# Splitting the two triangular row passes of the first mixer between VectorE and GpSimd

## The chip, the cores and the metric

The kernel runs on one core of one Trainium2 chip. The metric is the device time of one execution in microseconds, the median of several executions. The engines named below are TensorE (PE), VectorE (DVE), ScalarE (ACT), GpSimd (POOL) and the DMA queue of SyncE (SP).

## The reference, cut to what matters

The model is two layers of a mixer and a mixture of experts on a 1024 x 256 activation. Only the first mixer matters here, a delta rule over 512 tokens, 2 batches and 16 heads of 16 channels:

```
q = _l2norm(q) * Dk ** (-0.5)
k = _l2norm(k)
def step(S, inp):
    qt, kt, vt, bt = inp
    u = vt - einsum('bhk,bhkv->bhv', kt, S)
    S = S + bt[:, :, None, None] * kt[..., :, None] * u[..., None, :]
    o = einsum('bhk,bhkv->bhv', qt, S)
_, o = jax.lax.scan(step, S0, (qT, kT, vT, bT))
```

The output is normalised per head, gated, multiplied with `Wo` and added to `x`. Then come the experts of layer 0, an attention with 16 heads of 128 channels, and the experts of layer 1.

## The kernel before

The delta rule is computed in chunks of CH = 16 tokens. Inside a chunk the recurrence is a triangular system. Its matrices are built from products of the chunk's keys and queries (`grams`, TensorE) and turned so that the 128 partitions hold batch, tile and head, and the free dimension holds 8 chunks and the 16 x 16 entries. `scale_a` (L2760, VectorE) writes the scaled key-key entries `aul` from PSUM; ScalarE writes the query-key entries `pul` and the diagonal of the second matrix (L2439, L2446).

Then VectorE solves row by row:

- T is `ful[0]`. For i = 0 to 14, a multiplication (L2780) writes the products of column i of `aul` with row i of T into `tmp[0]`, and a subtraction (L2794) takes them from rows i+1 to 15. Each works on (15-i) x 8 x (i+1) elements per partition, between 120 and 512.
- The second matrix is `ful[1]`. For z = 1 to 15, a multiplication (L2788) writes the products of column z of `pul` with row z of T into `tmp[1]`, and an addition (L2798) adds them to rows z to 15, on (16-z) x 8 x z elements. Step z needs T's row z, which is final after T's step z-1.

The loop over m in `dve` runs T's step m and the second matrix's step m-2 together, as four instructions. An operand of all of them and the result lie in SBUF (`arena`, and `w` for the `tmp` buffers); none touches PSUM. `s_el` counts them, with the targets in `el_t` and `el_z`. Among the first three steps stand four pairs of `scale_a` and two `rke` (L2720); these read a PSUM bank and one SBUF operand.

TensorE meanwhile works through a written order: `turn_ft(i)` (L2251) turns four rows of T (i even) or of the second matrix (i odd) to the front, between the sums (L2131) and four `gates` (L2241). ScalarE takes the turned rows out (`ft_out`, L2469). `turn_ft(7)` needs the last row of the second matrix. Behind it VectorE copies two rows (L2805), and then VectorE, ScalarE and GpSimd spread the matrices (`spread`, L2820, L2501, L2645), TensorE forms `units` (L2287), and a serial chain over NCH = 32 chunks of the state follows (L2314, L2330, L2868), with no slack between its engines.

GpSimd's queue in that stretch holds, in this order: the clearing of `ful` (L2600, L2602), the scaling of `wo0` (L2610), the clearing of 4096 elements at XO (L2612, `s_qz`, on which 16 DMAs of SP wait, L2098), `hdiag` and `seed`, the chain's first state, in 16 small copies (L2614 to L2620), `wz` (L2626), two clearings that wait for the last gate (L2630, L2631), and the spreads.

Of the kernel before, what the change touches and what calls it, by code (L numbers as in the profile page):

```python
# [7 lines left out]
P = 128  # L8
# [3 lines left out]
KD = DIM // P  # L12
# [4 lines left out]
H0, D0, CONV = 16, 16, 4  # L17
CH = 16
# [34 lines left out]
ALU = mybir.AluOpType  # L53
# [1838 lines left out]
def make_attn0(nc, io, sem, sb, arena, bank, rest, g):  # L1892
# [14 lines left out]
    def at(off, n):  # L1907
        assert off + n <= ARENA
        return arena[:, off:off + n]
# [6 lines left out]
    XO = 10240 + 2 * XYW  # L1916
# [68 lines left out]
    s_el = sem("a0_el")  # L1985
    s_qz = sem("a0_qz")
# [90 lines left out]
    el_t, el_z, el_n = {}, {}, 0  # L2077
    for m in range(CH + 2):
        el_n += (m < CH - 1) + (1 <= m - 2)
        if m < CH - 1:  # L2080
            el_n += 1
            el_t[m] = el_n
        if 1 <= m - 2:
            el_n += 1
            el_z[m - 2] = el_n

    class Attn0:
# [12 lines left out]
        def pe(self, pe):  # L2100
# [144 lines left out]
            def turn_ft(i):  # L2245
                y, r0 = i % 2, i // 2 * 4
                pe.wait_ge(s_el, el_z[r0 + 3] if y else el_t[r0 + 2])
# [327 lines left out]
        def pool(self, pool):  # L2575
# [32 lines left out]
            pool.wait_ge(s_const.sem, n_const)  # L2608
            for k in range(KD):
                nc.gpsimd.tensor_scalar(wo0[:, k, :], wo0[:, k, :], norm_w[:, 0:1], 1.0, ALU.mult, ALU.mult).then_inc(s_one, 1)  # L2610
            pool.wait_ge(s_ut, 8)
            pool.memset(at(XO, 4096), 0.0).then_inc(s_qz, 1)  # L2612
# [75 lines left out]
        def dve(self, dve):  # L2688
# [78 lines left out]
            for m in range(CH + 2):  # L2767
                i, z = m, m - 2
                if m < 4:
                    scale_a(2 * m)  # L2770
                    scale_a(2 * m + 1)
                    if m in (1, 2):
                        rke(m + 1)
                    dve.wait_ge(s_ua, 2 * m + 2)
                if i < CH - 1:
                    n, w = CH - 1 - i, i + 1
                    tt = tmp[0][:, 0:n * 8 * w].rearrange("p (r c j) -> p r c j", r=n, c=8)
                    if m:
                        dve.wait_ge(s_el, el_t[m - 1])
                    nc.vector.tensor_tensor(tt, aul[:, i, :, i + 1:CH].rearrange("p c r -> p r c").unsqueeze(3).to_broadcast([P, n, 8, w]),  # L2780
                                            ful[0][:, i, :, 0:w].unsqueeze(1).to_broadcast([P, n, 8, w]),
                                            ALU.mult).then_inc(s_el, 1)
                if z >= 1:
                    nz = CH - z
                    tz = tmp[1][:, 0:nz * 8 * z].rearrange("p (r c j) -> p r c j", r=nz, c=8)
                    dve.wait_ge(s_el, el_z[z - 1] if z > 1 else el_t[z - 1])
                    dve.wait_ge(s_uz, 3 * (z // 4) + 3)
                    nc.vector.tensor_tensor(tz, pul[:, z, :, z:CH].rearrange("p c r -> p r c").unsqueeze(3).to_broadcast([P, nz, 8, z]),  # L2788
                                            ful[0][:, z, :, 0:z].unsqueeze(1).to_broadcast([P, nz, 8, z]),
                                            ALU.mult).then_inc(s_el, 1)  # L2790
                if i < CH - 1:
# [199 lines left out]
```

## Time and profile before

| what | us |
|---|---|
| median of 3 runs | 836.53 (835.92 to 839.29) |
| the profiled execution, its time | 836.49 |
| its span, first to last instruction | 834.7 |
| VectorE busy in the span | 482.1 |
| GpSimd busy in the span | 218.4 |
| mean granted TensorE clock | 0.991 |

All rows come from one profiled execution. A timeline row gives start, duration, engine, line of the kernel, operation, result and operands, their shapes and the count of merged instructions, and in brackets the idle time of the engine ahead of it with what ended it. A row of a windows view gives the stretch, its length, the busy time with the count in brackets, the granted TensorE clock as a share of 2.4 GHz, and DMA.

### The profile page before, as it was taken

How to read it: one execution, taken by the hardware profiler on the slowest of the kernel's cores; microseconds unless marked ns; L12 is line 12 of the kernel's file. 1: busy time of each engine (PE TensorE's matmuls, PEld its weight loads, DVE VectorE, ACT ScalarE, POOL GpSimd, SP SyncE). 2: the span in 40 equal slices, each digit the busy share in tenths (PEclk: the TensorE clock that was granted, in tenths of full speed). 3: DMA queues.
4: the chain of work that ended last, by engine and by line, in shares of the span. 5: the costliest groups of instructions: out<-in, count | busy, mean ns of one | idle time of the engine just before them, and what ended most of it. 6: DMA issues, size and time to landing. Idle time of an engine off the chain costs nothing.

```text
span 834.7 us, 14393 instructions
## 1 busy us (share of the span) xinstructions
PE 787.2 (94%) x4825; PEld 545.6 (65%) x4825; DVE 482.1 (58%) x1167; ACT 360.4 (43%) x755; POOL 218.4 (26%) x318
## 2 busy tenths in 40 slices
PE   5988799879989998899999999999999999999998
PEld 3576566665657776577777777777764545455557
DVE  5999866766622225865564575967645463324443
ACT  3988777646213324343323343232347666211111
POOL 3644654111610015111211211217712333200000
PEclk9998999999999999999999999999999999999999
DMA  4001790083343312034443232223333433284431
GB/s 145 2 1 29 220 309 1 3 209 101 102 139 103 106 60 82 13 103 135 122 131 93 69 102 69 61 54 99 119 71 114 141 96 110 88 278 126 127 126 50
DMA packets 95807, 85.72 MB, mean 103 GB/s; under 512 B 34792, under 2 KB 84456, under 8 KB 95736
## 3 DMA queue, kind: packets, MB, share of 16 engines
q1 hardware_dynamic: 88200, 70.05, 28.9%
q0 software_dynamic: 4224, 11.74, 4.0%
q10 hardware_dynamic: 3312, 3.02, 1.1%
q8 instruction: 41, 0.67, 0.3%
q14 instruction: 30, 0.25, 0.1%
HBM read 57.02 MB, written 26.71 MB: 100 GB/s over the span
## 4 chain that ended last, share of the span: by engine, by line
PE 79%; DVE 10%; ACT 6%; issue 3%; DMA 1%; SPq 1%; POOL 0%; ACTq 0%; DVEq 0%; POOLq 0%
PE bank L1502 9%; PE bank L1461 8%; PE bank L1320 7%; PE bank L1359 7%; PE bank L1345 6%; PE bank L1281 6%; PE bank L1297 6%; PE bank L744 4%; PE bank L770 3%; PE bank L967 3%; PE bank L2330 3%; PE bank L989 2%; ACT arena L2387 2%; PE bank L2287 2%; PE bank L2314 2%
## 5 line engine op out<-in xcount | busy, mean ns | idle before, releaser
L1619 ACT ACTIVATE arena<-bank 128x512 f32<-128x512 f32 (+1 forms) x96 | 46.8, 525 | 142.7 <-PE bank L1461 142.7
L1243 POOL TENSOR_TENSOR arena<-arena,causal_t 128x256 f32<-128x256 f32 x64 | 45.3, 729 | 208.5 <-ACT arena L1624 207.5
L1502 PEld LDWEIGHTS bank<-arena 128*128 128x128 f32 x640 | 76.2, 191 | 3.9 <-POOL arena L1243 2.3
L1502 PE MATMUL bank<-arena 128*128 128x129 f32 x640 | 77.0, 275 | 1.5 <-POOL arena L1243 1.5
L1461 PE MATMUL bank<-arena 128*128 128x512 f32 (+3 forms) x256 | 74.5, 434 | 1.4 <-DVE arena L1697 1.4
L1554 ACT ACTIVATE arena<-bank 128x512 f32<-128x512 f32 (+1 forms) x39 | 20.2, 520 | 120.7 <-PE bank L1281 111.9
L1320 PE MATMUL bank<-arena 128*128 128x256 f32 (+1 forms) x272 | 66.2, 382 | 3.5 <-DVE arena L1677 3.4
L1281 PE MATMUL bank<-xnT,arena 128*128 128x512 f32 (+1 forms) x168 | 65.9, 514 | 0.0
L1320 PEld LDWEIGHTS bank<-arena 128*128 128x128 f32 (+1 forms) x272 | 50.9, 190 | 21.8 <-issue 10.8
L1359 PEld LDWEIGHTS bank<-arena 128*128 128x128 f32 x256 | 48.3, 190 | 21.6 <-issue 13.6
L1359 PE MATMUL bank<-arena 128*128 128x256 f32 x256 | 60.8, 380 | 1.4 <-issue 0.9
L1345 PE MATMUL bank<-arena 128*128 128x512 f32 x128 | 60.5, 595 | 1.2 <-DVE arena L1695 0.8
L1297 PE MATMUL bank<-xnT,arena 128*128 128x512 f32 (+1 forms) x156 | 61.5, 516 | 0.0
L1461 PEld LDWEIGHTS bank<-arena 128*128 128x128 f32 x256 | 41.3, 191 | 27.0 <-issue 18.5
L1679 DVE TENSOR_TENSOR arena<-arena,bank 128x512 f32<-128x512 f32 (+1 forms) x25 | 15.6, 623 | 68.0 <-PE bank L1297 68.0
L851 POOL DMA_INDIRECT ret<-arena,ridx x32 | 30.7, 960 | 77.0 <-ACT arena L818 60.3
L1693 DVE TENSOR_TENSOR arena<-bank,arena 64x512 f32<-64x512 f32 x36 | 25.0, 693 | 36.7 <-PE bank L1345 26.2
L1297 PEld LDWEIGHTS bank<-xnT,arena 128*128 128x128 f32 x156 | 29.6, 190 | 25.3 <-issue 23.8
L744 PE MATMUL bank<-arena 128*64 (+1 forms) x256 | 44.9, 472 | 0.0
L1704 DVE COPY arena<-bank 128x256 f32<-128x256 f32 x64 | 24.1, 418 | 34.5 <-PE bank L1369 30.8
L2330 PE MATMUL bank<-w,arena 128*128 128x128 f32 x248 | 35.5, 286 | 7.2 <-DVE w L2863 3.3
L1281 PEld LDWEIGHTS bank<-xnT,arena 128*128 128x128 f32 x168 | 31.2, 190 | 16.5 <-issue 14.0
(297 smaller groups left out, 1489.6 us busy)
## 6 DMA issues: line engine op xcount, KB each, us to landing
arena<-in_w_gu SPq DMA_DIRECT2D x44, 256.0 KB, 3.3
rows_in<-place SPq DMA_DIRECT2D x5, 1664.0 KB, 14.6
arena<-in_w_dn SPq DMA_DIRECT2D x34, 128.0 KB, 3.5
rows<-arena SPq DMA_DIRECT2D x8, 544.0 KB, 4.4
arena<-in_w_dn SPq DMA_DIRECT2D x24, 176.0 KB
arena<-in_wq SPq DMA_DIRECT2D x32, 128.0 KB
arena<-in_wo SPq DMA_DIRECT2D x32, 128.0 KB
arena<-rows SPq DMA_DIRECT2D x32, 128.0 KB, 2.0
```

What stands on the lines that cost most here:

```text
L744: mm = nc.tensor.matmul(p_gu[J % 2][u * HR:(u + 1) * HR, 0:2 * FE].rearrange("p (y n) -> p y n", y=2), pxT[:, J % 2, k, u * HR:(u + 1) * H ...
L851: nc.gpsimd.indirect_dma_start(ret[h], bass.IndirectOffsetOnAxis(ap=ridx[:, h, j:j + 1], axis=0), py[J % NY], None).then_inc(s_ret, 16)
L1243: nc.gpsimd.tensor_tensor(blocks, blocks, causal_t[:].unsqueeze(1).to_broadcast([P, 2, P]), ALU.mult).then_inc(s_p, 1)
L1281: mm = nc.tensor.matmul(ring(M)[0][:, 0:n], (w_gu, w_gu1)[s][:, slot_of(M), k * P:(k + 1) * P], xnT[:, k, cols], start=(k == 0), stop=(k = ...
L1297: mm = nc.tensor.matmul(ring(M)[1][:, 0:n], (w_gu, w_gu1)[s][:, slot_of(M), (KD + k) * P:(KD + k + 1) * P], xnT[:, k, cols], start=(k == 0 ...
L1320: mm = nc.tensor.matmul(Y[s][half][l // 2][:, (l % 2) * DIM:(l % 2 + 1) * DIM], (hh, hh1)[s][rows, M % 3, j * P:(j + 1) * P], (w_dn, w_dn1 ...
L1345: mm = nc.tensor.matmul(b_q[:], wq[:, n % 2, k, :], xnT2[:, k, b * SEQ:(b + 1) * SEQ], start=(k == 0), stop=(k == KD - 1))
L1359: mm = nc.tensor.matmul(b_y[t // 2][:, (t % 2) * DIM:(t % 2 + 1) * DIM], oT[:, t * P:(t + 1) * P], wo[:, n % 2, :], start=first and t % 2 ...
L1461: mm = nc.tensor.matmul(b_s[sbank][:, o:o + w], kT[:, grp, kt * P:(kt + 1) * P], qr[:, kt * P:SEQ], start=True, stop=True, skip_group_chec ...
L1502: mm = nc.tensor.matmul(b_o[pair][:, t * (DH + 1):(t + 1) * (DH + 1)], pr[:, o:o + P], v[:, grp, kt, :], start=(kt == 0), stop=(kt == qb))
L1619: nc.scalar.activation(th[:, sbank * 512:sbank * 512 + w], b_s[sbank][:, 0:w], ACT.Tanh, scale=SCALE / SOFTCAP).then_inc(s_th, 1)
L2330: mm = nc.tensor.matmul(sacc[h][:, j * P:(j + 1) * P], kq[:, u, hq * P:(hq + 1) * P], ub[s][:, hq, :], start=False, stop=True, skip_group_ ...
```

## The change

VectorE runs all 15 steps of T first and then steps z = 8 to 15 of the second matrix. GpSimd runs steps z = 1 to 7, each as soon as T's row z is final, counted by the new semaphore `s_ez`. TensorE's `turn_ft(1)` and `turn_ft(3)` wait on `s_ez`. On GpSimd's queue, `hdiag` and `seed` move ahead of these steps and `seed` is made by 4 copies of 32 x 64 elements; the clearing at XO and the scaling of `wo0` move behind them.

```diff
-    el_t, el_z, el_n = {}, {}, 0
+    ZP = 7
+    el_t = {m: 2 * (m + 1) for m in range(CH - 1)}
+    el_z = {z: 2 * (CH - 1) + 2 * (z - ZP) for z in range(ZP + 1, CH)}
+    el_n = el_z[CH - 1]
...
             def turn_ft(i):
                 y, r0 = i % 2, i // 2 * 4
-                pe.wait_ge(s_el, el_z[r0 + 3] if y else el_t[r0 + 2])
+                if y and r0 + 3 <= ZP:
+                    pe.wait_ge(s_ez, 2 * (r0 + 3))
+                else:
+                    pe.wait_ge(s_el, el_z[r0 + 3] if y else el_t[r0 + 2])
...
-            pool.wait_ge(s_const.sem, n_const)
-            for k in range(KD):
-                nc.gpsimd.tensor_scalar(wo0[:, k, :], wo0[:, k, :], norm_w[:, 0:1], 1.0, ALU.mult, ALU.mult).then_inc(s_one, 1)
-            pool.wait_ge(s_ut, 8)
-            pool.memset(at(XO, 4096), 0.0).then_inc(s_qz, 1)
+            pool.wait_ge(s_pp, 12)
...
-                for x in range(4):
-                    ins = nc.gpsimd.tensor_copy(seed[rows, x * 64 + h * D0:x * 64 + (h + 1) * D0],
-                                                ident[rows, 32 * h + D0:32 * h + 32])
+                ins = nc.gpsimd.tensor_copy(seed[rows].rearrange("p (x h d) -> p x h d", x=4, d=D0)[:, :, h, :],
+                                            ident[rows, 32 * h + D0:32 * h + 32].unsqueeze(1).to_broadcast([32, 4, D0]))
             ins.then_inc(s_seed, 1)
+            pool.wait_ge(s_seed, 1)
+            for z in range(1, ZP + 1):
+                nz = CH - z
+                tz = tmp[1][:, 0:nz * 8 * z].rearrange("p (r c j) -> p r c j", r=nz, c=8)
+                pool.wait_ge(s_el, el_t[z - 1])
+                pool.wait_ge(s_uz, 3 * (z // 4) + 3)
+                if z > 1:
+                    pool.wait_ge(s_ez, 2 * (z - 1))
+                nc.gpsimd.tensor_tensor(tz, pul[:, z, :, z:CH].rearrange("p c r -> p r c").unsqueeze(3).to_broadcast([P, nz, 8, z]),
+                                        ful[0][:, z, :, 0:z].unsqueeze(1).to_broadcast([P, nz, 8, z]),
+                                        ALU.mult).then_inc(s_ez, 1)
+                pool.wait_ge(s_ez, 2 * z - 1)
+                dst = ful[1][:, z:CH, :, 0:z]
+                nc.gpsimd.tensor_tensor(dst, dst, tz, ALU.add).then_inc(s_ez, 1)
+            pool.wait_ge(s_ut, 8)
+            pool.memset(at(XO, 4096), 0.0).then_inc(s_qz, 1)
+            pool.wait_ge(s_const.sem, n_const)
+            for k in range(KD):
+                nc.gpsimd.tensor_scalar(wo0[:, k, :], wo0[:, k, :], norm_w[:, 0:1], 1.0, ALU.mult, ALU.mult).then_inc(s_one, 1)
```

In `dve` the loop over m becomes a loop over i with T's two instructions, then a wait for `s_ez` at 14 and for `s_uz` at 12, and a loop over z from 8 with the second matrix's two.

VectorE, where T's step 8 stood beside the second matrix's step 6, before: `arena` operands are `aul`, `pul` and `ful`, `w` is `tmp`.

```order
L2780 TENSOR_TENSOR w<-arena 128x504 [waits a0_el]
L2788 TENSOR_TENSOR w<-arena 128x480 [waits a0_uz,a0_el]
L2794 TENSOR_TENSOR arena<-arena,w 128x56x9 [waits a0_el]
L2798 TENSOR_TENSOR arena<-arena,w 128x80x6 [waits a0_el]
L2780 TENSOR_TENSOR w<-arena 128x480 [waits a0_el]
```

The same place after, and the turn from T's last step to the second matrix's step 8:

```order
L2791 TENSOR_TENSOR w<-arena 128x504 [waits a0_el]
L2796 TENSOR_TENSOR arena<-arena,w 128x56x9 [waits a0_el]
L2791 TENSOR_TENSOR w<-arena 128x480 [waits a0_el]
...
L2796 TENSOR_TENSOR arena<-arena,w 128x8x15 [waits a0_el]
L2803 TENSOR_TENSOR w<-arena 128x512 [waits a0_el,a0_uz,a0_ez]
L2808 TENSOR_TENSOR arena<-arena,w 128x64x8 [waits a0_el]
```

The pairs of two passes became one pass behind the other, and each instruction now waits for the one ahead of it. 14 instructions left VectorE.

GpSimd, from the scaling of `wo0` to the clearing of `ub`, before:

```order
L2610 TENSOR_SCALAR wo<-wo,norm_w 128x256 [waits s_const]
L2610 TENSOR_SCALAR wo<-wo,norm_w 128x256
L2612 MEMSET arena 128x4096 [waits a0_ut]
L2613 MEMSET hdiag 128x64
...
L2620 COPY w<-ident 32x16 x4
L2626 TENSOR_TENSOR wz<-kn,beta 128x128 [waits a0_srk,a0_rk,a0_seed]
L2630 MEMSET w 128x1024 [waits a0_g,a0_b,a0_srk]
```

After, from the last copy of `seed` on:

```order
L2614 COPY w<-ident 32x4x16
L2625 TENSOR_TENSOR w<-arena 128x120 [waits a0_uz,a0_el,a0_seed]
L2630 TENSOR_TENSOR arena<-arena,w 128x120 [waits a0_ez]
...
L2625 TENSOR_TENSOR w<-arena 128x504 [waits a0_ez,a0_uz,a0_el]
L2630 TENSOR_TENSOR arena<-arena,w 128x72x7 [waits a0_ez]
L2632 MEMSET arena 128x4096 [waits a0_ut]
L2635 TENSOR_SCALAR wo<-wo,norm_w 128x256 [waits s_const]
L2635 TENSOR_SCALAR wo<-wo,norm_w 128x256
L2639 TENSOR_TENSOR wz<-kn,beta 128x128 [waits a0_srk,a0_rk,a0_seed]
L2643 MEMSET w 128x1024 [waits a0_g,a0_b,a0_srk]
```

Fourteen two-operand instructions now stand ahead of the clearing at XO, and the scaling of `wo0` stands behind both.

## Rows read from the trace of the kernel before

**Rows 1.** The page: the chain that ended last, shares of the span by engine.
```profile
PE 79%; DVE 10%; ACT 6%; issue 3%; DMA 1%; SPq 1%; POOL 0%; ACTq 0%; DVEq 0%; POOLq 0%
```

**Rows 2.** The chain that ended last: start, us, what; from the solve's end to the units.
```profile
90.08 0.67 PE bank L2251 x4
...
90.77 0.60 DVE arena L2805
...
91.92 1.34 DVE arena L2820 x3
...
93.58 1.07 PE bank L2287 x16
...
97.98 1.11 PE bank L2287 x16
```

**Rows 3.** Windows view of VectorE: L2780, L2794, then the last eight of L2788.
```profile
62.20:90.10 27.90, 7.05 (x12) 0.88 0.24 39
...
62.20:90.10 27.90, 6.91 (x12) 0.88 0.24 39
...
77.45:90.10 12.65, 4.33 (x8) 0.80 0.52 84
```

**Rows 4.** Timeline of VectorE in the solve.
```profile
62.23 0.56 DVE L2780 TENSOR_TENSOR w<-arena 128x384 f32<-128x384 f32 x1
...
65.65 0.65 DVE L2780 TENSOR_TENSOR w<-arena 128x480 f32<-128x480 f32 x1
...
74.78 0.92 DVE L2780 TENSOR_TENSOR w<-arena 128x480 f32<-128x480 f32 x1
...
87.53 0.48 DVE L2788 TENSOR_TENSOR w<-arena 128x312 f32<-128x312 f32 x1
88.05 0.48 DVE L2798 TENSOR_TENSOR arena<-arena,w 128x312 f32<-128x312 f32 x1
```

**Rows 5.** Timeline of GpSimd beside the solve.
```profile
52.91 0.93 POOL L2610 TENSOR_SCALAR wo<-wo,norm_w 128x256 f32<-128x256 f32 x2
59.73 3.52 POOL L2612 MEMSET arena<- 128x4096 f32 x1 [5.89 <-PE bank L2196]
...
69.09 2.14 POOL L2620 COPY w<-ident 32x16 f32<-32x16 f32 x4
74.57 0.61 POOL L2626 TENSOR_TENSOR wz<-kn,beta 128x128 f32<-128x128 f32 x1 [3.35 <-ACT kn L2459]
```

**Rows 6.** Timeline near 197 us, VectorE first, then GpSimd.
```profile
196.99 0.89 DVE L575 TENSOR_TENSOR arena<-arena 128x32 f32<-128x32 f32 x1
197.92 0.43 DVE L582 TENSOR_TENSOR arena<-arena 128x256 f32<-128x256 f32 x1
198.38 1.38 DVE L585 TENSOR_TENSOR arena<-arena 128x256 f32<-128x256 f32 x1
...
196.78 1.06 POOL L2661 TENSOR_TENSOR arena<-arena 128x512 f32<-128x512 f32 x1 [2.28 <-DVE arena L2901]
197.91 1.56 POOL L2665 TENSOR_TENSOR arena<-arena,xn 128x512 f32<-128x512 f32 x1
```

**Rows 7.** Timelines of TensorE, ScalarE and SP's queue at the solve's end.
```profile
88.82 1.04 PE L2251 MATMUL bank<-ident,arena 128*128 128x128 f32 x8
...
89.52 2.37 ACT L2469 COPY arena<-bank 128x512 f32<-128x512 f32 x3
...
76.72 10.70 SPq L2098 DMA_DIRECT2D arena<-arena  x16
```

**Rows 8.** Windows view: PE, PEld, DVE, ACT, POOL busy, PEclk, DMA share, GB/s.
```profile
48.00:52.00 4.00, 2.11 (x56) 1.75 (x59) 3.86 (x8) 3.98 (x9) 1.97 (x2) 0.97 0.02 4
52.00:56.00 4.00, 4.00 (x38) 3.62 (x31) 3.76 (x8) 2.52 (x4) 1.79 (x19) 0.60 0.01 2
...
76.00:80.00 4.00, 4.00 (x19) 3.95 (x20) 3.93 (x8) 2.69 (x5) 0.00 (x0) 0.50 0.37 56
...
96.00:100.00 4.00, 2.14 (x32) 1.00 (x32) 3.74 (x14) 2.59 (x9) 4.00 (x8) 1.00 1.05 354
```

More of the change, by code:

```diff
@@ L1985, in make_attn0 @@
     s_el = sem("a0_el")
+    s_ez = sem("a0_ez")
     s_qz = sem("a0_qz")
@@ L2073, in xy_from @@
         return xy_bank(i)[:].rearrange("p (q y v c i) -> p q y v c i", q=2, y=2, v=2, c=4)[:, :, y, :, :, :]
-    el_t, el_z, el_n = {}, {}, 0
[L2078 to L2085, printed above, removed]
+    ZP = 7
+    el_t = {m: 2 * (m + 1) for m in range(CH - 1)}
+    el_z = {z: 2 * (CH - 1) + 2 * (z - ZP) for z in range(ZP + 1, CH)}
+    el_n = el_z[CH - 1]
     class Attn0:
@@ L2766, in dve @@
             dve.wait_ge(s_pz, 4)
[L2767 to L2791, printed above, removed]
-                    dve.wait_ge(s_el, el_t[m] - (1 if z >= 1 else 0) - 0 - (0 if z >= 1 else 1))
-                    dst = ful[0][:, i + 1:CH, :, 0:w]
-                    nc.vector.tensor_tensor(dst, dst, tt, ALU.subtract).then_inc(s_el, 1)
-                if z >= 1:
-                    dve.wait_ge(s_el, el_z[z] - 1 - (1 if i < CH - 1 else 0))
-                    dst = ful[1][:, z:CH, :, 0:z]
-                    nc.vector.tensor_tensor(dst, dst, tz, ALU.add).then_inc(s_el, 1)
@@ new lines, in dve @@
+            for i in range(CH - 1):
+                if i < 4:
+                    scale_a(2 * i)
+                    scale_a(2 * i + 1)
+                    if i in (1, 2):
+                        rke(i + 1)
+                    dve.wait_ge(s_ua, 2 * i + 2)
+                n, w = CH - 1 - i, i + 1
+                tt = tmp[0][:, 0:n * 8 * w].rearrange("p (r c j) -> p r c j", r=n, c=8)
+                if i:
+                    dve.wait_ge(s_el, el_t[i - 1])
+                nc.vector.tensor_tensor(tt, aul[:, i, :, i + 1:CH].rearrange("p c r -> p r c").unsqueeze(3).to_broadcast([P, n, 8, w]),
+                                        ful[0][:, i, :, 0:w].unsqueeze(1).to_broadcast([P, n, 8, w]),
+                                        ALU.mult).then_inc(s_el, 1)
+                dve.wait_ge(s_el, el_t[i] - 1)
+                dst = ful[0][:, i + 1:CH, :, 0:w]
+                nc.vector.tensor_tensor(dst, dst, tt, ALU.subtract).then_inc(s_el, 1)
@@ new lines, in dve @@
+            dve.wait_ge(s_ez, 2 * ZP)
+            dve.wait_ge(s_uz, 12)
+            for z in range(ZP + 1, CH):
+                nz = CH - z
+                tz = tmp[1][:, 0:nz * 8 * z].rearrange("p (r c j) -> p r c j", r=nz, c=8)
+                dve.wait_ge(s_el, el_z[z] - 2)
+                nc.vector.tensor_tensor(tz, pul[:, z, :, z:CH].rearrange("p c r -> p r c").unsqueeze(3).to_broadcast([P, nz, 8, z]),
+                                        ful[0][:, z, :, 0:z].unsqueeze(1).to_broadcast([P, nz, 8, z]),
+                                        ALU.mult).then_inc(s_el, 1)
+                dve.wait_ge(s_el, el_z[z] - 1)
+                dst = ful[1][:, z:CH, :, 0:z]
+                nc.vector.tensor_tensor(dst, dst, tz, ALU.add).then_inc(s_el, 1)
```

## The prediction, written before the change was timed

> **What bounds the kernel now.** I read the shares of the chain of waits first, then the chain between 86 and 101 us, and then the timelines of the engines there. TensorE holds 79% of the chain [rows 1], but not in this stretch: between 62 and 90 us VectorE steps through the solve almost without a pause. Of 27.9 us from the first four-instruction step at 62.23 on, all but a few tenths are its instructions [rows 3, 4]. The reader should see in the chain how the solve ends: TensorE's last turn starts at 90.08, right behind the last addition; VectorE's copy of two rows follows, and the spreads start at 91.92 [rows 2]. From there the units and the serial chain of the state follow, so what these spreads gain or lose the kernel gains or loses in full.
>
> Just under that chain lies a second one. TensorE's turns 5 and 6 run at 88.82, behind the last gate, and ScalarE's last three copies run from 89.52 to 91.89 without a pause [rows 7]. The spreads wait for the third. So if VectorE ended its solve several us sooner, these two engines would still hold the spreads at about 91.9. This caps any gain at about nothing.
>
> **VectorE's own work after the change.** From 62.23 on, twelve steps of T are left. Their multiplications took 7.05 us, of which one was lengthened from 0.65 to 0.92 (below), so 6.78; the subtractions took 6.91 [rows 3, 4]. Two instructions that depend on each other start 0.04 us after the other's end (87.53 and 0.48, then 88.05) [rows 4], and now all do: 24 x 0.04 = 0.96. T would end at 62.23 + 6.78 + 6.91 + 0.96 = 76.9. Steps 8 to 15 of the second matrix: 4.33 us for the multiplications, as much for the additions, 16 x 0.04 of gaps, 9.3 together [rows 3]. That gives 86.2 with nothing in the way, against 90.0 before: 3.8 us less. The 14 instructions that left held more than that, but the interleaved order let independent ones overlap, and this is lost.
>
> **What stands in the way: GpSimd's reads.** Twice the trace shows VectorE reading two SBUF operands while GpSimd does so too. At 74.57 GpSimd multiplied 128 elements for `wz`, and the multiplication of 480 elements beside it took 0.92 instead of 0.65 us [rows 4, 5]: 0.27 us, or 2.1 ns per element of GpSimd's. At 197.91 GpSimd ran 512 elements, and VectorE's 256 elements took 1.38 us [rows 6], where the 256 just ahead of them took 0.43: 0.95 us, or 1.9 ns per element. At 196.99 VectorE's 32 elements took 0.89 and ended with GpSimd's 512 [rows 6]. From 0.43 for 256 and 0.65 for 480 I estimate 0.2 for 32 elements alone, so it stood for 0.7 us, 1.4 ns per element, a lower bound since GpSimd had started before. So VectorE stands for nearly the time in which GpSimd works, rather than sharing. The copies of 32 x 16 elements did it no visible harm though they took longer themselves (0.53 us each in the last four) [rows 5]; they are too small to serve as a price.
>
> The moved steps have 120 + 224 + 312 + 384 + 440 + 480 + 504 = 2464 elements, twice: 4928. At 1.9 ns that is 9.4 us. I take 1.9 and not 2.1 because the 512-element row is the nearer one in size. The first three of the fourteen (464 elements, 0.9 us) can run beside `scale_a` and `rke`, which read PSUM and one SBUF operand; I take 1.1 off with a part of the fourth. The rest meets T: from z = 4 on, each GpSimd instruction finds a VectorE one beside it, and both take turns. This leaves **8.3 us**. Bounds: 1.4 ns gives 6.7 - 0.7 = 6.0; 3.0 ns, the whole of the 1.56 us for 512 elements [rows 6], gives 15.0 - 1.4 = 13.6.
>
> The Trainium skill ("SBUF — State Buffer", section "Who interferes with whom") says that a VectorE instruction with two SBUF inputs contends with a GpSimd instruction that reads SBUF, and that the second to start fully blocks until the first is done. The rows above agree with the blocking, but charge somewhat less than the whole GpSimd instruction; by the letter of the page the sum would move toward the 13.6.
>
> **The rest of GpSimd's queue.** `hdiag` and `seed` run before the solve needs GpSimd: the scaling of `wo0` that stood there took 0.93 us [rows 5] and the moved items are writes and four small copies, some 2 to 2.5 us from 52.9, done by about 55.5, while `scale_a` and T's first step lie between there and 62.23. They cost nothing, and win nothing, since the chain uses `seed` first behind the spreads. The scaling of `wo0` now meets VectorE: two instructions of 256 elements with one operand, 0.93 together. I charge 0.6 (0 to 0.93). `wz` is charged its 0.27 as before. The clearing at XO (3.52 us, writes only) [rows 5] ended at 63.2 and will end at about 81: T's step 7 ends at 69 undisturbed and at about 77 with the charge, GpSimd's z = 7 with it. SP's 16 DMAs wait for it, 10.70 us from 76.72 on [rows 7], so they now run from 81 to 92 and have landed by 95; the first reader (L2832) stands behind the first units, which started at 93.58 and will start past 98. That is hidden, with some 4 us to spare. The waits on `s_ez` in turns 1 and 3 are met on time: turn 3 stands two gates of TensorE ahead of the turns at 88.82, and step 7 is done at about 77.
>
> **Sum.** 86.2 + 8.3 + 0.6 + 0.3 = 95.4 for the end of the solve. Turns 5 and 6 and their copies are then long done or nearly, so the tail is shorter: TensorE's last turn 0.05 + 0.67, VectorE's copy of two rows 0.60 [rows 2], spreads at 96.75. Before it was 91.92. **Later by 4.8 us.**
>
> **TensorE's clock.** Between 48 and 52 us TensorE was busy 2.11 of 4 us, and then the granted clock fell to half, 1.2 GHz (0.60 over the next stretch); between 76 and 80 it stood at 0.50 again. Between 96 and 100, with 2.14 of 4 busy, it did not fall [rows 8]. After the change TensorE has nothing from 89 to about 91.6 (turn 5 waits for z = 11), two turns, nothing to 95.4, one turn and the seed's products, and then the units: some 3 us of work in 9. That is less than ahead of the fall at 52, so I expect a fall at about 93 and the first units at half clock. The four groups of units start at 93.58 to 97.98 and take 1.07 each [rows 2]; at half clock they take 2.14, against a distance of about 1.5. Two slow groups cost 0.9 us, three 2.0; TensorE was slow for some 4 us after the fall at 52. **I take 1.5** (0 to 3).
>
> **Total**: 836.49 for the profiled execution + 4.8 + 1.5 = 842.8. The profiled execution lies 0.04 below the median of 836.53, so the sum stands for both. The forecast is 842.8 us, 0.75% slower.
>
> **Rivals.**
> - Reads collide, the clock holds. Same sum without the last term: 841.3. For it speaks the stretch at 96 to 100 us. At the low price of 1.4 ns it would be 839.0.
> - GpSimd's instructions block as a whole, or VectorE always goes first and GpSimd ends behind T. The first is 13.6 in place of 8.3: 846.6 with the clock still up, 848.1 with it down. The second: T ends at 76.9, GpSimd still has some 10 us of its 12 to do, and steps 8 to 15 add 9.3 after 87 to 88: the spreads start at about 98, or 843 to 844. The `wz` row speaks against it, since GpSimd got in there.
> - No collision worth the name. Then VectorE is done at 86.5, and the spreads wait for TensorE's turn 7, which comes right behind turns 5 and 6 at 89.86, and for ScalarE's last copy at 91.9. The time is 836.5. This is the case on the other side: the mechanism is that the shared work is hidden and TensorE and ScalarE become the bound. It decides if GpSimd's instructions hold VectorE for less than 91.2 - 86.5 = 4.7 us in all, about 1 ns per element. Against it stand three rows at 1.4 to 2.1 ns.
> - Faster by over 0.5% would need 4.2 us from somewhere in or behind the spreads. Nothing in the rows offers that.
>
> **How the numbers follow.** Forecast (collision, clock down) 0.46; clock holds 0.25; the larger price or GpSimd behind T 0.12; no collision 0.14; anything else, a gain among it, 0.03. About 0.5%, 4.2 us, is what a measurement of this kernel can tell from no change. The forecast's case lies above 840.7 nearly whole, the second for about two thirds, the third whole: slower 0.74. The no-collision case and the low end of the second give same 0.23, and faster has 0.03. The range of 838.0 to 848.0 leaves out the no-collision case, the remainder, and the top of the third, some 0.2 together; its low end takes in most of the lower price, its high end the whole-instruction price with the clock down.
>
> **What the changed profile would show.** Right: VectorE's T instructions between 62 and 77 us take 1.2 to 1.6 us each instead of 0.55 to 0.69, with GpSimd's fourteen of 0.4 to 1.6 us between them; T's last eight steps and steps 8 to 15 have the old durations; the spreads start near 96.8; SP's sixteen DMAs start near 81; the granted clock is at 0.5 somewhere between 92 and 102. Wrong: T's instructions keep their 0.55 to 0.69 (no collision), a wait of VectorE for GpSimd ahead of step 8 (GpSimd behind T), the first reader at XO waiting for a DMA, or a clock of 1.00 throughout. The forecast fails most easily in the price per element, since 0.5 ns in it are 2.5 us.

## The result: 0.45% slower

The changed kernel takes 840.11 us (median of 18 runs), the kernel before 835.39 us (18 runs). The ratio is 1.0045, 95% interval 1.0034 to 1.0055, or 3.8 us (2.8 to 4.6); the two medians by themselves lie 4.7 us apart, and I go by the ratio. One execution of the changed kernel took 1614.58 us, for a reason that the record does not show, and is left out of the ratio. The span of the profiled execution is 838.2 us, TensorE's mean granted clock 0.988. I had forecast 842.8 in a range of 838.0 to 848.0: the sign and the range held, and the sum was 2.5 us too high (6.3 us of loss instead of 3.8).

VectorE beside GpSimd, the timeline after, where steps 7 to 9 of T meet GpSimd's z = 6 and 7; then the end of the solve, the copy of two rows and the spreads. Columns as in [rows 4].

```profile
73.95 1.51 DVE L2791 TENSOR_TENSOR w<-arena 128x512 f32<-128x512 f32 x1
75.50 1.54 DVE L2796 TENSOR_TENSOR arena<-arena,w 128x512 f32<-128x512 f32 x1
77.07 1.54 DVE L2791 TENSOR_TENSOR w<-arena 128x504 f32<-128x504 f32 x1
78.65 0.68 DVE L2796 TENSOR_TENSOR arena<-arena,w 128x504 f32<-128x504 f32 x1
...
82.06 0.71 DVE L2791 TENSOR_TENSOR w<-arena 128x384 f32<-128x384 f32 x1
...
95.30 0.28 DVE L2808 TENSOR_TENSOR arena<-arena,w 128x120 f32<-128x120 f32 x1
...
96.79 0.65 DVE L2815 COPY arena<-bank 128x256 f32<-128x256 f32 x1 [0.54 <-PE bank L2250]
97.53 3.78 DVE L2830 TENSOR_SCALAR arena<-arena,headmask 128x256 f32<-128x256 f32 x9
101.51 1.33 DVE L2830 TENSOR_SCALAR arena<-arena,headmask 128x256 f32<-128x256 f32 x3 [0.20 <-PE bank L2286]
```

The same timeline for GpSimd; these rows answer to [rows 5].

```profile
56.48 0.24 POOL L2614 COPY w<-ident 32x64 f32<-32x64 f32 x1
...
75.08 1.41 POOL L2625 TENSOR_TENSOR w<-arena 128x504 f32<-128x504 f32 x1 [0.17 <-POOL arena L2630]
76.56 1.51 POOL L2630 TENSOR_TENSOR arena<-arena,w 128x504 f32<-128x504 f32 x1
78.01 3.52 POOL L2632 MEMSET arena<- 128x4096 f32 x1
81.50 1.62 POOL L2635 TENSOR_SCALAR wo<-wo,norm_w 128x256 f32<-128x256 f32 x2
```

The collision is plain. While GpSimd's multiplication and addition of 504 elements run, each of VectorE's instructions takes 1.51 to 1.54 us, as forecast (1.2 to 1.6). As soon as GpSimd goes over to a clearing, which reads nothing, the same 504 elements take 0.68. Beside the scaling of `wo0`, 384 elements take 0.71 instead of 0.56 [rows 4].

TensorE at the end of the solve, and SP's sixteen transfers; these answer to [rows 2, 7].

```profile
91.92 1.09 PE L2250 MATMUL bank<-ident,arena 128*128 128x128 f32 x8 [0.96 <-DVE arena L2808]
95.63 1.12 PE L2250 MATMUL bank<-ident,arena 128*128 128x128 f32 x4 [2.62 <-DVE arena L2808]
97.50 2.08 PE L2296 MATMUL bank<-w,ident 128*128 128x256 f32 x4 [0.75 <-ACT arena L2468]
99.50 4.53 PE L2286 MATMUL bank<-arena 128*32 128x256 f32 x64
105.54 0.69 PE L2313 MATMUL bank<-sh,arena 128*64 128x64 f32 x16 [1.50 <-DVE sh L2855]
```

```profile
81.56 10.69 SPq L2094 DMA_DIRECT2D arena<-arena  x16
```

The windows of that stretch after, which answer to [rows 8]:

```profile
92.00:96.00 4.00, 1.38 (x10) 1.14 (x11) 3.76 (x10) 1.93 (x2) 0.31 (x2) 0.81 0.22 37
96.00:100.00 4.00, 3.25 (x16) 1.79 (x18) 3.37 (x8) 3.14 (x8) 2.40 (x5) 0.50 0.51 137
100.00:104.00 4.00, 4.00 (x64) 1.89 (x56) 3.73 (x13) 3.34 (x10) 3.08 (x7) 0.83 0.97 314
```

TensorE's clock falls to half behind turn 6 and comes back inside the units: turn 7 takes 1.12 us instead of 0.67 [rows 2], the seed's products 2.08. That too was forecast. But from the first spread to the chain's first product at 105.54 it takes 8.01 us; before, it was 8.43 (100.35, the start of L2314 there, less 91.92 [rows 2]). The fall cost nothing there.

**Where the 3.8 us are.** The solve starts at a different moment in each profiled execution: the first pair of `scale_a` at 55.75 before, at 57.20 after. TensorE's clock falls near 50 us in both, but not at the same point of its work, and nothing that the change touches stands ahead of it. So I count from that pair. The pair before, then after:

```profile
55.75 0.81 DVE L2760 TENSOR_TENSOR arena<-bank,wul 128x256 f32<-128x256 f32 x2
...
57.20 0.74 DVE L2773 TENSOR_TENSOR arena<-bank,wul 128x256 f32<-128x256 f32 x2
```

| from the first `scale_a` pair to | before | after | difference | forecast |
|---|---|---|---|---|
| end of the solve | 34.27 | 38.38 | +4.1 | +5.4 |
| first spread | 36.17 | 40.33 | +4.2 | +4.8 |
| first product of the chain | 44.60 | 48.34 | +3.7 | +6.3 |
| first projection behind the layer (L1281) | 136.63 | 140.36 | +3.7 | +6.3 |

The difference is complete when the chain begins and stays to the layer's end; it is the 3.8 us of the ratio, within 0.1. The spans differ by 3.5 although the pair comes 1.45 us later after the change: what lies behind the layer took 642.3 us before and 640.6 after. That part varies by itself: it is 641.0 us in the repetition of the changed kernel (e9 below) and 642.5 in e1.

### The profile page after: what moved, and what is told of

The parts are those of the page before. It is cut to its first block, busy times and chain, and to the rows that moved or that the text cites. A ratio compares the mean times of both kernels' runs of the same rounds, so it can differ in the third digit from the quotient of the medians.

```text
span 838.2 us, 14374 instructions
## 1 busy us (share of the span) xinstructions
PE 789.9 (94%) x4825; PEld 547.4 (65%) x4825; DVE 485.3 (58%) x1153; ACT 360.8 (43%) x755; POOL 228.7 (27%) x320
## 4 chain that ended last, share of the span: by engine, by line
PE 78%; DVE 11%; ACT 5%; issue 3%; DMA 1%; SPq 0%; POOL 0%; ACTq 0%; DVEq 0%; POOLq 0%
PE bank L1502 9%; PE bank L1461 8%; PE bank L1320 7%; PE bank L1359 6%; PE bank L1345 6%; PE bank L1281 6%; PE bank L1297 6%; PE bank L744 4%; PE bank L770 3%; PE bank L967 3%; PE bank L2329 3%; PE bank L989 2%; PE bank L2286 2%; PE bank L2313 2%; PE bank L1369 2%
## 5 line engine op out<-in xcount | busy, mean ns | idle before, releaser
L1281 PE MATMUL bank<-xnT,arena 128*128 128x512 f32 (+1 forms) x168 | 65.9, 515 | 0.0
L1281 PEld LDWEIGHTS bank<-xnT,arena 128*128 128x128 f32 x168 | 31.3, 190 | 16.4 <-issue 13.9
```

The lines of the kernel that those rows point to most:

```text
L1281: mm = nc.tensor.matmul(ring(M)[0][:, 0:n], (w_gu, w_gu1)[s][:, slot_of(M), k * P:(k + 1) * P], xnT[:, k, cols], start=(k == 0), stop=(k = ...
```

## The experiments

Eleven kernels beside the changed one. "From pair to layer" is the last row of the table above, taken from each one's profiled execution.

| kernel | median us (runs) | kernel before, timed beside it | ratio, 95% interval | from pair to layer |
|---|---|---|---|---|
| changed | 840.11 (18) | 835.39 | 1.0045 (1.0034 to 1.0055) | 140.4 |
| e1_all_on_dve | 840.30 (10) | 835.62 | 1.0050 (1.0033 to 1.0067) | 140.1 |
| e2_write_only | 834.68 (10) | 835.62 | 0.9982 (0.9959 to 1.0005) | 136.5 |
| e3_pool_behind_T | 846.19 (2) | 835.62 | 1.0119 (1.0062 to 1.0176) | 147.4 |
| e4_products_in_psum | 836.90 (10) | 835.62 | 1.0010 (0.9991 to 1.0028) | 137.2 |
| e5_filled_clock | 847.27 (6) | 838.57 | 1.0091 (1.0063 to 1.0120) | 146.3 |
| e6_first_state_early | 837.76 (10) | 838.57 | 0.9982 (0.9953 to 1.0010) | 136.5 |
| e8_psum_interleaved | 837.05 (10) | 838.57 | 0.9981 (0.9957 to 1.0006) | 137.2 |
| e12_psum_interleaved_sums_early | 838.79 (10) | 838.57 | 1.0007 (0.9985 to 1.0029) | 137.1 |
| e9_changed_again | 838.51 (9) | 836.15 | 1.0031 (1.0013 to 1.0049) | 140.4 |
| e10_half_filler | 839.82 (4) | 836.15 | 1.0050 (1.0031 to 1.0069) | 140.5 |
| e11_interleaved | 838.79 (8) | 836.15 | 1.0031 (1.0015 to 1.0047) | 139.6 |

### Is it the collision, and how large is it?

**e1_all_on_dve**: the changed kernel without GpSimd's share.

```diff
-    ZP = 7
+    ZP = 0
-            dve.wait_ge(s_ez, 2 * ZP)
```

> VectorE runs T first and then all fifteen steps of the second matrix; GpSimd has none. Collision theory: nobody stands in the way, so T's steps from the fourth on take 14.7 us and the fifteen steps some 17.2 us (the 9.3 of steps 8 to 15, and 7.9 for steps 1 to 7); the solve ends some 4 us later than before and the spreads start 3.5 to 4 us later: the time is 3 to 4 us above before, the same as the changed kernel within 0.7 us, since what GpSimd took over came back as waiting. Rival (GpSimd's share is worth something and the loss of the changed kernel comes from the order or the clock): this kernel is 3 us or more slower than the changed one.

It costs what the changed kernel costs: 1.0050 against 1.0045. VectorE ends the solve at 95.28, 38.85 us after its pair, 0.5 later than in the changed kernel, though it has fourteen instructions more and no collision. So giving seven steps away bought 0.5 us at the solve's end, and nothing where the chain begins (48.10 us behind the pair in e1, 48.34 after the change).

e1 shows one thing more. VectorE runs the same sixty instructions of the solve as in the kernel before, only T first and the second matrix behind it, and ends 4.6 us later (38.85 against 34.27), since each instruction now waits for the one ahead of it. Some 0.3 us of this come from the scaling of `wo0`, which now stands beside the solve; the order itself costs some 4.3. So the 4.1 us by which the changed kernel ends its solve later are a sum: the new order costs 4.3, the small instructions of GpSimd 0.2, the fourteen instructions that left give back 8.0 (their time and gaps in e1, 78.05 to 86.03 us), and the collision, weighed below at 7.6, takes nearly all of that again. The collision is why the move did not pay; the loss against the kernel before is about as large as the price of the order.

**e2_write_only**: GpSimd's fourteen instructions become clearings of the same elements, so steps 1 to 7 of the second matrix are left out.

```diff
-                nc.gpsimd.tensor_tensor(tz, pul[:, z, :, z:CH].rearrange("p c r -> p r c").unsqueeze(3).to_broadcast([P, nz, 8, z]),
-                                        ful[0][:, z, :, 0:z].unsqueeze(1).to_broadcast([P, nz, 8, z]),
-                                        ALU.mult).then_inc(s_ez, 1)
+                nc.gpsimd.memset(tmp[1][:, 0:nz * 8 * z], 0.0).then_inc(s_ez, 1)
-                nc.gpsimd.tensor_tensor(dst, dst, tz, ALU.add).then_inc(s_ez, 1)
+                nc.gpsimd.memset(dst, 0.0).then_inc(s_ez, 1)
```

> The changed kernel with GpSimd's fourteen two-operand instructions replaced by clearings of the same shapes, which write and read nothing (the second matrix is left wrong by it). Collision by reads: T's instructions keep 0.28 to 0.69 us, the solve ends at about 87 us of the trace, TensorE's and ScalarE's chain of gates holds the spreads at about 92 plus whatever the start of the trace is late, and the time is that of before within 1 us. Rival (GpSimd's presence, its writes or its semaphores cost): T's instructions stay lengthened to over 1 us and the time stays 3 us or more above before.

Its timeline at the solve's end: VectorE, and ScalarE's last copies.

```profile
86.14 0.28 DVE L2806 TENSOR_TENSOR arena<-arena,w 128x120 f32<-128x120 f32 x1
...
89.98 0.58 DVE L2813 COPY arena<-bank 128x256 f32<-128x256 f32 x1 [2.89 <-PE bank L2250]
91.53 2.78 DVE L2828 TENSOR_SCALAR arena<-arena,headmask 128x256 f32<-128x256 f32 x6 [0.96 <-ACT arena L2468]
```

```profile
89.17 2.33 ACT L2468 COPY arena<-bank 128x512 f32<-128x512 f32 x3
```

Without GpSimd's reads VectorE is done 31 us after the pair (86.42 less 55.43), 7.4 us sooner than in the changed kernel, and then waits 2.89 us for TensorE and 0.96 us for ScalarE. The spreads start 36.1 us behind the pair, as in the kernel before (36.2). This is the rival "no collision" made real, and it gives the time that it gave: no change. So even a helper that did not hold VectorE up would have won nothing here, because TensorE's turns and ScalarE's copies end right behind.

**e3_pool_behind_T**: GpSimd waits until T is done.

```diff
-                pool.wait_ge(s_el, el_t[z - 1])
+                pool.wait_ge(s_el, el_t[CH - 2])
```

> GpSimd's steps wait until T is done, so neither engine reads SBUF beside the other. Collision theory: T's steps keep their old durations (14.7 us from the fourth on), and the fourteen GpSimd instructions show what they need alone: 0.2 us and 1.7 to 2.1 ns per element, some 12 to 13 us in all; VectorE waits for them, and the time is 7 to 9 us above before. If the lengthening in the changed kernel were slow GpSimd code and not waiting, the fourteen would take as long here as there (some 15.7 us).

GpSimd's last pair with nothing beside it, and VectorE's first instruction behind it:

```profile
90.44 1.16 POOL L2625 TENSOR_TENSOR w<-arena 128x504 f32<-128x504 f32 x1 [0.17 <-POOL arena L2630]
91.69 1.16 POOL L2630 TENSOR_TENSOR arena<-arena,w 128x504 f32<-128x504 f32 x1
```

```profile
92.88 0.69 DVE L2803 TENSOR_TENSOR w<-arena 128x512 f32<-128x512 f32 x1 [14.72 <-POOL arena L2630]
```

This weighs the collision. T's twelve steps from i = 3 take 14.55 us here (63.61 to 78.16), within 0.1 of the forecast's 14.65; in the changed kernel 21.92 (64.26 to 86.18). Of the 7.37 us between them, 0.31 belong to `wo0` and 0.14 to `wz`; some 0.64 more lie in steps 1 and 2, ahead of i = 3. So GpSimd's fourteen cost VectorE 7.6 us, or **1.5 ns per element of GpSimd's** (7.6 / 4928). GpSimd's own fourteen last 12.97 us alone and 15.67 in the changed kernel. VectorE therefore stood for somewhat over half of GpSimd's time: for 504 elements 0.85 us (1.54 less 0.69) of 1.16. GpSimd's 504 elements take 0.54 and 0.67 us more in e3 than its 120 (1.16 against 0.62 and 0.49). By my estimate its time so grows by 1.4 to 1.7 ns per element on top of a fixed 0.3 to 0.45 us, and the 1.5 ns that VectorE stood are about the growing part alone. The solve ends 7.0 us later than in the changed kernel, and the layer 7.0; I had expected 7 to 9 us over the kernel before and found 10: VectorE waits 14.72 us, not 12.97, since some 0.1 us pass between each two of GpSimd's dependent instructions, 1.75 us in all.

**e4_products_in_psum**: the work stays where the change put it, but T's products from i = 5 on lie in a free PSUM bank.

```diff
-                tt = tmp[0][:, 0:n * 8 * w].rearrange("p (r c j) -> p r c j", r=n, c=8)
+                tt = (bank[3] if i >= 5 else tmp[0])[:, 0:n * 8 * w].rearrange("p (r c j) -> p r c j", r=n, c=8)
+                if i == 5:
+                    dve.wait_ge(s_siv, KD + 4)
```

> The changed kernel, but T's products of steps 5 to 14 go to a PSUM bank. The subtractions then read one SBUF operand and one PSUM operand. Collision by two SBUF reads: the subtractions keep 0.6 to 0.7 us beside GpSimd, only the multiplications wait, and the delay from step 5 on falls from some 7 to 2 or 3 us: the time is 3 to 4 us under the changed kernel. Rival (any overlap of the two engines in SBUF costs, by writes or bandwidth): the subtractions stay at 1.3 to 1.5 us, and the time is the changed kernel's within 0.7 us.

VectorE in e4, and GpSimd beside it:

```profile
69.97 0.80 DVE L2793 TENSOR_TENSOR bank<-arena 128x504 f32<-128x504 f32 x1
70.81 0.68 DVE L2798 TENSOR_TENSOR arena<-arena,bank 128x504 f32<-128x504 f32 x1
71.52 0.76 DVE L2793 TENSOR_TENSOR bank<-arena 128x512 f32<-128x512 f32 x1
72.31 0.69 DVE L2798 TENSOR_TENSOR arena<-arena,bank 128x512 f32<-128x512 f32 x1
```

```profile
71.89 1.40 POOL L2625 TENSOR_TENSOR w<-arena 128x480 f32<-128x480 f32 x1 [0.17 <-POOL arena L2630]
73.37 1.47 POOL L2630 TENSOR_TENSOR arena<-arena,w 128x480 f32<-128x480 f32 x1
```

The subtraction of 512 elements takes 0.69 beside GpSimd, where it took 1.54, since one of its operands is in PSUM now. The multiplication still reads two operands in SBUF. The first one behind the change of place took 1.28 us (480 elements at 67.97), the later ones only 0.76 to 0.81. There VectorE's multiplication starts ahead of GpSimd's (71.52 against 71.89), so the two seem to have fallen into step. That this order is the reason is argued, not shown: GpSimd's 480 elements take 1.40 us here, but 1.38 in the changed kernel too, against 1.13 alone in e3. With the place of the products alone changed (the multiplication writes them, the subtraction reads them), 3.2 of the 3.7 us come back at the layer's end. At the solve's end it is somewhat over half of the collision: 34.16 us behind the pair, against 38.38 in the changed kernel and 30.99 in e2; the rest is hidden under ScalarE's copies (the last three run from 91.38 to 93.73, the first spread starts at 93.76). Together with e2, where GpSimd writes as much and VectorE is not held, this settles the cause: the reads collide, not the writes, the work or the waits. The Trainium skill ("SBUF — State Buffer", section "Who interferes with whom") says the same: an instruction of VectorE with at most one SBUF input, outside its two-port modes, does not contend with GpSimd (0.69 us here), and GpSimd only writing does not contend with two inputs either (e2). The page also calls the shared ports an exclusive lock; its sentence that the other engine is blocked for the whole instruction stands in that section for the two-port modes, and in the page's section "Terms" for the shared ports in general. For these instructions that is too strong in size: 0.85 of 1.16 us above, and in the changed kernel one instruction of VectorE's and one of GpSimd's pass every 1.5 to 1.6 us, less than the 0.69 and 1.16 that they take alone, 1.85 together.

### Does the fall of TensorE's clock cost anything?

**e5_filled_clock**: twenty products of the identity with itself between turns 6 and 7.

```diff
             for i in range(5, 8):
                 turn_ft(i)
+                if i == 6:
+                    for _ in range(20):
+                        nc.tensor.matmul(bank[3][:, 0:P], ident[:], ident[:], start=True, stop=True, skip_group_check=True)
```

> The changed kernel with 20 more TensorE matmuls of 128 columns into a bank nobody reads, between turns 6 and 7, so that TensorE isn't idle there. As the prediction had it (the clock's fall costs 1.5 us): the granted clock stays at 1.00 to the units, and the time is 1 to 2 us under the changed kernel. Rival, from comparing the traces of before and after (the units wait for the spreads, and spreads that start later collide less with GpSimd): the clock stays up, and the stretch from the spreads' start to the chain's first matmul is 8.4 us as before instead of 8.0, so the time is that of the changed kernel or up to 0.5 us above it.

TensorE in e5, then its windows in the chain:

```profile
91.54 4.63 PE L2268 MATMUL bank<-ident 128*128 128x128 f32 x40
96.01 0.60 PE L2250 MATMUL bank<-ident,arena 128*128 128x128 f32 x4
```

```profile
106.00:108.00 2.00, 2.00 (x32) 1.12 (x29) 0.88 (x3) 0.68 (x3) 2.00 (x5) 0.54 1.09 388
...
114.00:116.00 2.00, 2.00 (x12) 1.78 (x8) 0.42 (x1) 0.00 (x0) 0.00 (x0) 0.50 1.07 376
```

The filler was too long (4.63 us) and delayed turn 7 by itself. The clock then held through turn 7 and the units, and fell twice inside the chain instead, where every product is waited for: the chain took 96.3 us instead of 92. So this run says little of the fall ahead of the units and much of falls behind them: the two together cost some 4 us there. This is one execution, the slowest of the six (850.44 us). The filler was too large for the question; e10 below has half of it, with the changed kernel timed beside it.

**e9_changed_again**: the changed kernel once more.

> The changed kernel once more, beside the two kernels of this call and on their chip. Every theory expects what was measured: 3 to 4.5 us above the kernel before, the solve ending 5 to 6 us later after scale_a's start than before, turn 7 at half clock (1.1 us), and some 8 us from the first spread to the first product of the chain.

**e10_half_filler**: as e5 with `range(10)`.

> The changed kernel with 10 matmuls of 128 columns of the identity into a bank that is free, between turns 6 and 7 on TensorE. They take 2.3 us by the 4.63 us of twenty, and TensorE's pause there was 2.62 us, so turn 7 is not delayed as it was with twenty. Theory A, the fall of TensorE's clock ahead of the units costs 1.5 us of the time, as predicted: with the clock kept up this kernel is 1 to 1.5 us faster than the changed kernel of this call. Theory B, the units wait for the spreads and the fall costs at most turn 7's own 0.4 to 0.5 us: the time is that of the changed kernel within 0.5 us, and the stretch from the first spread to the chain's first product is as long as before (8.4 us) although the units run at full clock.

TensorE in e10 (each product is listed as two matmuls), from the filler to the chain's first product:

```profile
91.60 2.40 PE L2268 MATMUL bank<-ident 128*128 128x128 f32 x20
94.38 0.66 PE L2250 MATMUL bank<-ident,arena 128*128 128x128 f32 x4 [0.39 <-DVE arena L2811]
95.80 1.13 PE L2299 MATMUL bank<-w,ident 128*128 128x256 f32 x4 [0.76 <-ACT arena L2471]
97.50 2.29 PE L2289 MATMUL bank<-arena 128*32 128x256 f32 x32 [0.57 <-DVE arena L2833]
100.16 1.07 PE L2289 MATMUL bank<-arena 128*32 128x256 f32 x16 [0.38 <-issue]
101.90 1.07 PE L2289 MATMUL bank<-arena 128*32 128x256 f32 x16 [0.67 <-issue]
104.27 0.69 PE L2316 MATMUL bank<-sh,arena 128*64 128x64 f32 x16 [1.30 <-DVE sh L2858]
```

The changed kernel reproduced: 140.4 us from pair to layer, turn 7 in 1.11 us, 8.00 us from first spread to chain. In e10 the clock is 1.00 in every window from 90 to 116 us. Turn 7 is back at 0.66, and the stretch is back at 8.43: 0.45 won, 0.43 lost, and 140.5 us from pair to layer. Its ratio is no better than that of e9 (1.0050 against 1.0031, the intervals overlap), and its median of four runs is 1.3 us above e9's, more than the 0.5 us that theory B allowed; the traces do not show that difference, and theory A, which asked for 1 to 1.5 us less, is excluded. At full clock TensorE pauses 0.38 and 0.67 us between the groups of units. The profile names no releaser for these pauses, but VectorE's twelfth spread ends at 101.80 and the last group starts at 101.90, so it waits for the spreads. In the changed kernel these pauses are gone and the groups end no later for the chain. Why the stretch is even 0.4 us shorter then, I can only argue: VectorE's twelve spreads take 3.78 + 1.33 us in the changed kernel and 5.96 in e10, so they may collide less when the last three are held back, as they are there until the first group of units is done (`s_xy`).

### Parts of the change, and the order

**e6_first_state_early**: the kernel before with only GpSimd's queue in the new order: `hdiag` and `seed` (in four copies) ahead, the clearing at XO and the scaling of `wo0` behind.

```diff
+            pool.wait_ge(s_pp, 12)
+            nc.gpsimd.memset(hdiag[:], 0.0).then_inc(s_pz, 1)
+            nc.gpsimd.memset(seed, 0.0).then_inc(s_pz, 1)
...
+            pool.wait_ge(s_seed, 1)
             pool.wait_ge(s_ut, 8)
             pool.memset(at(XO, 4096), 0.0).then_inc(s_qz, 1)
+            pool.wait_ge(s_const.sem, n_const)
+            for k in range(KD):
+                nc.gpsimd.tensor_scalar(wo0[:, k, :], wo0[:, k, :], norm_w[:, 0:1], 1.0, ALU.mult, ALU.mult).then_inc(s_one, 1)
```

> The kernel before with one part of the change alone: the first state by four copies, ahead; the clearing at XO and the scaling of wo0 behind them. Expected: the scaling of wo0 lengthens VectorE's solve by 0.2 to 0.4 us in place of nothing, and of this nothing reaches the spreads, since TensorE and ScalarE hold them 0.5 us longer; time of before within 0.5 us. Rival (the order of GpSimd's queue matters by itself): over 1 us from before, either way.

No change, 136.5 us from pair to layer. This part neither costs nor wins, as its term in the sum had it.

**e11_interleaved**: the changed kernel, VectorE's two passes in turn again where both are its own (z from 8).

> The changed kernel with the order of VectorE's instructions alone undone: T's step m and the second matrix's step m-2 in turn where both are VectorE's (z from 8), GpSimd keeps z = 1 to 7 with its operands in SBUF. Theory: T's steps 10 to 14 overlap with z = 8 to 12, so that 10 to 14 dependences of 0.04 us and some waits go, worth 0.4 to 1 us against the changed kernel; the collision stays. Rival, the loop order is what costs, not the collision: the time returns to the kernel before, 3 to 4 us less.

The solve ends 36.70 us behind the pair, 1.7 us sooner than in the changed kernel, more than I had expected. But only 0.8 reach the layer's end:

```profile
94.19 0.66 PE L2257 MATMUL bank<-ident,arena 128*128 128x128 f32 x4 [2.12 <-DVE arena L2820]
95.60 2.07 PE L2303 MATMUL bank<-w,ident 128*128 128x256 f32 x4 [0.75 <-ACT arena L2475]
97.60 5.76 PE L2293 MATMUL bank<-arena 128*32 128x256 f32 x64
```

The clock falls here at the end of turn 7, near 95.1 us (0.77 over 94 to 96, then 0.50 up to 100), and comes back only near 101.9, 6.3 us behind the first spread. The units meet nearly all of the slow time: 5.76 us for 64 instead of 4.53, and 9.36 us from first spread to chain, 0.9 more than at full clock. What counts is how far the half clock reaches behind the first spread, not how near ahead of it the fall comes. In e1 the fall comes nearer still, 0.2 us ahead of the first spread at 96.80, but the clock is back at 100.0, 3.2 us behind it, and the stretch is the shortest of all, 7.73 us. In the changed kernel the clock is back 3.8 us behind the first spread (8.01), in e9 4.2 (8.00). The windows of e11, then of e1:

```profile
100.00:102.00 2.00, 2.00 (x24) 0.92 (x20) 1.90 (x7) 1.54 (x5) 2.00 (x5) 0.53 1.00 308
```

```profile
96.00:98.00 2.00, 1.24 (x3) 1.07 (x4) 1.87 (x4) 1.88 (x4) 1.13 (x3) 0.65 0.31 109
...
100.00:102.00 2.00, 2.00 (x44) 1.07 (x40) 2.00 (x7) 2.00 (x7) 1.45 (x3) 1.00 0.90 287
```

In the time e11 equals e9 (838.79 and 838.51); a gain of 0.8 us is within their scatter. Its order is the old one only from T's step 10 on, so it does not test what the whole order costs; e1 does, some 4.3 us at the solve's end.

**e8_psum_interleaved**: both, e4's bank and e11's order.

> T's products of steps 5 to 14 in a PSUM bank, and steps 8 to 15 of the second matrix interleaved with T's steps 10 to 14 as before, GpSimd with steps 1 to 7. The interleaving gives back some 1 us, so VectorE ends its solve about 1 us earlier than with the PSUM products alone. If TensorE and ScalarE hold the spreads, as the run with writes only showed, less than 0.3 us of this reaches the time: before within 1 us. If VectorE is still the bound, the time is 0.8 to 1.2 us under the PSUM products alone.

VectorE ends the solve 33.3 us behind its pair, 1 us sooner than in the kernel before, and nothing of it arrives: the spreads wait for ScalarE's last of three copies (2.32 us from 89.95), and pair to layer is 137.2. This is the cap of e2 again, in a kernel that computes everything. It even lies 0.5 us later, with the first spread 36.7 us behind the pair: TensorE's last gate, too, starts 31.9 us behind it, against 31.3 before.

**e12_psum_interleaved_sums_early**: e8, with the query sums of TensorE moved from between turns 0 and 1 into the key-query products, to lift that cap. VectorE's scaling of these sums (`qn`, 0.27 us) moves ahead of the spreads with them.

```diff
                 mm.then_inc(s_kqm, 1)
+                if u == 5:
+                    pe.wait_ge(s_siv, KD + 4)
+                    sums(sq[1], s_sqq, bank[2], s_ssq, (0,))
+                if u == 7:
+                    sums(sq[1], s_sqq, bank[2], s_ssq, (1,))
...
             turn_ft(0)
-            sums(sq[1], s_sqq, bank[6], s_ssq)
             turn_ft(1)
```

> The same, with the 32 matmuls of the query sums moved ahead into TensorE's waits for ScalarE, in another bank. TensorE then reaches its last turns some 3 to 4 us sooner and no longer holds the spreads; VectorE's end does. Expected: spreads 1 to 2.5 us earlier than in the kernel before, time 1 to 2 us under before. If what was gained is given back behind the spreads, the time equals before within 0.5 us.

The expected 1 to 2 us did not come. The chain does start sooner, 43.62 us behind the pair instead of 44.60. Its steps keep that 1 us to the 30th of 32 (its first product at 186.11 less 57.41, against 185.43 less 55.75), and then lose it. The windows of that stretch, the kernel before and then e12:

```profile
181.00:191.00 10.00, 9.10 (x105) 8.29 (x104) 5.59 (x17) 5.21 (x15) 2.33 (x2) 1.00 0.93 252
```

```profile
181.00:191.00 10.00, 9.31 (x96) 8.43 (x96) 4.66 (x16) 3.97 (x15) 2.32 (x2) 0.83 0.91 233
```

TensorE's clock drops for a while at the end of the chain in e12 and not before; the last two steps take 1.4 us longer, and the sum is 137.1. That is one execution; whether it is the rule for this kernel stays open, but the timed runs show no gain either.

## The prediction, step by step

- **What bounds the kernel, and the cap.** Right, as e2 and e8 show: with VectorE done 3.3 and 1.0 us earlier than before the spreads still wait for TensorE's turn and ScalarE's copy.
- **VectorE's own work.** Right. T's steps from i = 3 took 14.55 us where I had 14.65, steps 8 to 15 took 9.26 (86.32 to 95.58) where I had 9.3. What the prediction did not draw from it is how much of the fourteen instructions' 8.0 us the lost overlap takes: some 4.3, by e1.
- **The collision.** Right in kind, a little large in size: 7.6 us against 8.3, 1.5 ns per element against 1.9. The best row was the one that I kept as a lower bound, 1.4 ns from the 0.89 us instruction [rows 6]. The small terms were 0.31 for `wo0` against 0.6, and 0.14 for `wz` against 0.27. Together 8.0 us against 9.2. The lower bound has a slip in it: 4928 elements at 1.4 ns are 6.9 us, not 6.7, so it is 6.2 and not 6.0. The measured 7.6 lies between it and the 8.3.
- **The rest of GpSimd's queue.** Right: `seed` done at 56.7, the clearing at 81.5, the transfers landed at 92.3 with no reader waiting, and e6 without effect. Turns 1 and 3 did not wait.
- **The tail.** I had 1.35 us from the solve's end to the spreads; it was 1.95. I had put the fall of the clock at 93 us and then priced turn 7, which starts after that, at full clock: 0.45 us forgotten. The rest is 0.05 in VectorE's copy and 0.1 in the gaps around it.
- **TensorE's clock.** The step that failed. The fall came, within 1.5 us of the moment forecast, but the 1.5 us charged for it did not: 0.0 in the stretch as a whole, turn 7 included (e10). I multiplied the slow groups' excess over their distance, 2.14 against 1.5, without asking who sets that distance (and two slow groups come to 1.3 us by that working, not 0.9). The pauses between the groups [rows 2] were TensorE's own waiting for spreads, and at half clock its work grew into them before it delayed anything (e10). The row that I had for "slow for some 4 us" came from another place; here half clock lasted from about 94.5 to 101.4 (0.81 over 92 to 96, 0.83 over 100 to 104), and five of these seven us had passed when the units began at 99.50.
- **The sum.** 6.3 us forecast. Less 1.2 (collision and small terms too large), less 1.9 (the clock's 1.5 and the 0.4 by which the stretch was shorter), plus 0.6 (tail) gives 3.8, the measured value. The two large misses have the same sign, so little of the result is owed to errors that cancel. But the range of 10 us is wide: it holds the sum without the clock's term (841.3) as well as with it, so that the time fell into it says nothing for the clock.
- **The rivals.** The prediction called 4.2 us, 0.5%, the least that can be told from no change; the 0.45% measured lies just under that, on the side to which it had given 0.23, though 18 runs a side leave no doubt of the sign (1.0034 to 1.0055). The clock as a cost was wrong, so the second case, 841.3, described it better, though for another reason than the one it gave: the clock did not hold. GpSimd ending behind T did not occur (its last addition ended at 78.07, T at 86.18); e3 shows what it would have cost. "No collision" is excluded by the timeline, and e2 shows that its time was worked out rightly.

## To carry to other kernels

Before handing work of VectorE to GpSimd, look at where both find their operands: if VectorE's instructions beside it read two SBUF operands, price each element of GpSimd's at about 1.5 ns of VectorE's time (f32, two operands, 120 to 504 elements here), as much as VectorE would have needed for the work itself; with T's products in PSUM somewhat over half of that went away. Price the order, too: running the two passes one behind the other instead of in turn cost some 4.3 us with no helper at all (e1). Find the second chain just below the critical one first, since it decides what any relief can be worth. And charge a slower clock only where the slowed engine has no pauses: half clock up to 3.2 to 4.2 us behind the first spread cost that stretch nothing, up to 6.3 us behind it 0.9 us, and two falls inside the serial chain some 4 us.

## What the hardware showed that I had not expected

- Two engines that collide need not cost each other the same each time. In e4 VectorE's multiplication with two SBUF operands took 0.76 to 0.81 us beside GpSimd where it started ahead of GpSimd's (0.69 alone, 1.28 for the first), while in the changed kernel it took 1.51. That the order of starting decides is my reading; no run changes it alone.
- The stretch behind the spreads was 0.4 to 0.7 us shorter with TensorE at half clock for its first 3.2 to 4.2 us (8.00 in e9, 7.73 in e1) than at full clock (8.43 in e10 and before, 8.44 in e4).
- Work that only keeps TensorE busy can move a fall of the clock rather than avoid it: e5 kept it up at 94 us and had it fall at 106 and at 113 us, where it cost more. Half of that work, in e10, kept the clock at 1.00 up to 116 us.
